# Second cross attention of a two-layer gated block: negated row maxima rounded to bf16 and carried by DMA, copies moved from VectorE to ScalarE, half-transposes and chunks rescheduled, 16 leading matmuls removed

## The reference, cut to what matters

```python
# second cross attention: keys and values from the context, queries from the normalised x
v = values.reshape(N, -1, 16, 16) @ Wv.T
k = keys.reshape(N, 77, 16, 16) @ Wk.T
q = queries.reshape(N, 1024, 16, 16) @ Wq.T
energy = einsum('bqhd,bkhd->bhqk', q, k)
energy = where(mask, energy, -1e20)
attn = softmax(energy / 4, axis=-1)
out = einsum('bhqk,bkhd->bqhd', attn, v).reshape(N, 1024, 256) @ Wo.T + bo
x = x + tanh(g) * out
```

## Time and profile before

| | us |
|---|---|
| median of three runs | 1420.08 |
| lowest and highest | 1419.99, 1422.82 |
| profiled execution, its own time | 1424.06 |
| its span, first to last instruction | 1422.3 |
| TensorE busy, share of the span | 1264.7, 89% |
| VectorE busy | 1044.8, 73% |
| ScalarE busy | 854.3, 60% |
| GpSimd busy | 160.5, 11% |

### The profile page before, as it was taken

One profiled execution on the slowest core, in us unless ns is written; L12 is line 12 of the kernel. 1 busy time (PEld: TensorE's weight loads), 2 busy tenths in 40 slices (PEclk: granted clock), 3 DMA queues, 4 the chain that ended last, 5 costly groups with the idle time before them and its releaser, 6 DMA issues.

```text
span 1422.3 us, 26541 instructions
## 1 busy us (share of the span) xinstructions
PE 1264.7 (89%) x10690; PEld 590.5 (42%) x10690; DVE 1044.8 (73%) x1563; ACT 854.3 (60%) x1432; POOL 160.5 (11%) x139
## 2 busy tenths in 40 slices
PE   4898974899899899948899999999999999999988
PEld 3566662454455755514433233232322333233237
DVE  4897494666664756545699999999999999999802
ACT  2233472666665155511287877887887787887871
POOL 2220021110600223310600000000000000000000
PEclk8977985999999999978799999999999999999999
DMA  5000026444450013340524443323443323443003
GB/s 177 24 1 14 1 29 111 95 85 89 90 90 2 0 67 133 134 94 11 82 50 69 82 79 57 75 54 64 82 81 62 67 56 63 82 81 48 2 1 118
DMA packets 78825, 92.56 MB, mean 65 GB/s; under 512 B 15210, under 2 KB 53356, under 8 KB 78704
## 3 DMA queue, kind: packets, MB, share of 16 engines
q1 hardware_dynamic: 78704, 90.87, 31.6%
HBM read 67.02 MB, written 23.80 MB: 64 GB/s over the span
## 4 chain that ended last, share of the span: by engine, by line
PE 58%; DVE 28%; ACT 7%; issue 4%; DMA 1%; SPq 1%; POOL 1%; DVEq 0%; ACTq 0%; POOLq 0%
DVE sm L1971 18%; PE ps L1460 9%; PE ps L1451 8%; PE ps L1432 6%; PE ps L1351 4%; ACT W L964 3%; PE ps L1216 2%; PE ps L1250 2%; PE ps L1570 2%; PE ps L1167 2%; PE ps L1358 2%; PE ps L1241 2%; PE ps L1299 1%; PE ps L1442 1%; PE ps L1387 1%
## 5 line engine op out<-in xcount | busy, mean ns | idle before, releaser
L1971 DVE TENSOR_REDUCE sm<-ps 128x1 f32<-128x1024 f32 x512 | 599.8, 1218 | 33.1 <-PE ps L1432 29.8
L964 ACT ACTIVATE W<-ps 128x512 f32<-128x512 f32 x1024 | 534.8, 604 | 140.2 <-PE ps L1460 136.3
L1460 PE MATMUL ps<-R 99*32 99x512 bf16 x4096 | 318.5, 383 | 6.2 <-ACT W L964 3.2
L1451 PE MATMUL ps<-W,R 128*32 128x512 f32 x2048 | 266.4, 596 | 0.7 <-ACT W L964 0.7
L1460 PEld LDWEIGHTS ps<-R 99*32 99x32 bf16 x4096 | 86.2, 94 | 225.4 <-ACT W L964 168.5
L882 ACT CAST R<-ps 4x2048 bf16<-4x2048 f32 x32 | 59.5, 1858 | 80.7 <-PE ps L1216 80.7
L1776 DVE TENSOR_REDUCE small<-ps 128x4 f32<-128x308 f32 x128 | 60.9, 477 | 62.6 <-PE ps L1205 62.2
L1432 PE MATMUL ps<-R 50*128 50x512 bf16 x512 | 89.2, 389 | 15.6 <-DVE sm L1971 12.9
L1432 PE MATMUL ps<-KM,R 50*128 50x512 bf16 x512 | 87.2, 384 | 9.6 <-DVE sm L1971 6.6
L1451 PEld LDWEIGHTS ps<-W,R 128*32 128x32 f32 x2048 | 63.2, 111 | 42.5 <-ACT W L964 1.4
L765 POOL COPY R<-R 128x512 f32<-128x512 f32 x16 | 10.3, 644 | 591.7 <-PE ps L1451 591.7
(11 more groups left out here) (258 smaller groups left out, 1587.1 us busy)
## 6 DMA issues: line engine op xcount, KB each, us to landing
R<-x_parts SPq DMA_DIRECT2D x96, 128.0 KB, 4.8
R<-q_parts SPq DMA_DIRECT2D x192, 64.0 KB
R<-q_parts SPq DMA_DIRECT2D x96, 128.0 KB
R<-k_parts SPq DMA_DIRECT2D x96, 128.0 KB
x_parts<-R SPq DMA_DIRECT2D x8, 768.0 KB, 4.1
q_parts<-R SPq DMA_DIRECT2D x24, 256.0 KB, 2.6
k_parts<-R SPq DMA_DIRECT2D x24, 256.0 KB, 2.6
X<-in_x SPq DMA_DIRECT2D x4, 1024.0 KB, 9.8
```

Of the source, the lines that this page charges most:

```text
L964: act.activation(PR[:, s % 2, h, :], third_bank("score", 64 * u + n), ACT.Exp, scale=0.25).then_inc(s_sfree, 1)
L1451: mm = pe.matmul(bank(7)[32 * h:32 * h + 32, :], VST[j][:, k, h, :], PR[:, s % 2, h, :], start=(k == 0), stop=(k == TB - 1))
L1460: mm = pe.matmul(o[32 * c:32 * c + 32, :], KST[j][0:MAX_ROW + 1, h, t:t + 32], QST[j][0:MAX_ROW + 1, h, 512 * (s // 8):512 * (s // 8) + 51 ...
L1971: dve.tensor_reduce(MX[:, half, h, q:q + 1], bank(2 * ((p + 1) % 2), 2), AX, ALU.max).then_inc(s_tfree, 1)
```

## The change

- The negated maxima `Mn` are written as bf16, and `max_transposes1` multiplies them with the bf16 identity in place of the float32 one (four matmuls of 128 columns, as before).
- ScalarE's `max_rows1` copies the 4 x 512 numbers once, to a small double buffer `mrow1`, and then issues four DMAs of 1 KB, each of which brings one head's row to partition 96 of the stack. It waits for its own copy before it issues, and the wait for the stack's readers stands in front of the DMAs. `scores1` waits for the landing of these DMAs (64 on a semaphore of its own) and not for the copy. The stacks have 97 rows in place of 100, and the one-hot rows of `K1s` become one row of ones (one memset in place of four copies on VectorE).
- `copy_out1` moves from VectorE to ScalarE, behind the exponentials and ahead of `max_rows1`.
- On TensorE `max_transposes1(m + 2)` stands ahead of `out_transposes1(m - 2)`.
- The half-transposes of the last eight halves come two steps earlier (steps 0 to 3, 6 to 9, 14 to 17 in place of 0 to 3, 8 to 11, 16 to 19), and three layernorm chunks two steps earlier as well (steps 0, 4, 6, 12, 14 in place of 0, 6, 8, 14, 16).
- The 16 matmuls ahead of the first step are gone.

```diff
-        SR1 = SR + 4
+        SR1 = SR + 1
+        mrow1 = R2f[SR:SR + 4, 5434:5946].bitcast(BF16).rearrange("p (u n) -> p u n", u=2)
-        Mn = small[:, 464:528].rearrange("p (u q j) -> p u q j", u=2, q=8)
+        Mn = small[:, 464:496].bitcast(BF16).rearrange("p (u q j) -> p u q j", u=2, q=8)
+        HALVES = {max(0, 8 * (i // 4) - 2) + i % 4: FIRST + i for i in range(12)}
+        CHUNKS = {0: 3, 4: 4, 6: 5, 12: 6, 14: 7}
...
             def max_rows1(m):
                 act.wait_ge(s_mt, m + 1)
+                if m >= 2:
+                    act.wait_ge(s_mrl[m % 2], 64 * (m // 2))
+                act.copy(mrow1[:, m % 2], bank(2)[SR:SR + 4, :]).then_inc(s_mrc, 1)
                 if m >= 6:
                     act.wait_ge(s_sc, 4 * (m - 5))
-                act.copy(Xs[m // 2 % 3][SR:SR1, :, 512 * (m % 2):512 * (m % 2) + 512],
-                         bank(2)[SR:SR1, :].unsqueeze(1).to_broadcast([4, 4, 512])).then_inc(s_mrc, 1)
+                act.wait_ge(s_mrc, m + 1)
+                for j in range(4):
+                    act.dma_start(Xs[m // 2 % 3][SR:SR1, j, 512 * (m % 2):512 * (m % 2) + 512],
+                                  mrow1[j:j + 1, m % 2]).then_inc(s_mrl[m % 2], 16)
...
+                if m >= 1:
+                    copy_out1(m - 1)
                 if m + 2 < 2 * UNITS:
                     max_rows1(m + 2)
...
-                pe.wait_ge(s_mrc, m + 1)
+                pe.wait_ge(s_mrl[m % 2], 64 * (m // 2 + 1))
...
-            keep_warm(4, 16)
             for m in range(2 * UNITS):
                 scores1(m)
                 if m >= 1:
                     values1(m - 1)
+                if m + 2 < 2 * UNITS:
+                    max_transposes1(m + 2)
                 if m >= 2:
                     out_transposes1(m - 2)
-                if m + 2 < 2 * UNITS:
-                    max_transposes1(m + 2)
...
-            for g in range(4):
-                sel = dve.tensor_copy(K1s[SR:SR1, 4 * g:4 * g + 4, :],
-                                      identB[SR:SR1, SR:SR1].unsqueeze(2).to_broadcast([4, 4, B * KX]))
-            sel.then_inc(s_mk1, 1)
+            dve.memset(K1s[SR:SR1, :, :], 1.0).then_inc(s_mk1, 1)
```

More of the change, by code:

```diff
@@ L247, in build_program @@
         s_mrc = sem("max1_rows")
+        s_mrl = [sem(f"max1_rows_loaded{n}") for n in range(2)]
         s_sc = sem("scores1")
@@ L266, in build_program @@
         FIRST = 4
+        HALVES = {max(0, 8 * (i // 4) - 2) + i % 4: FIRST + i for i in range(12)}
+        CHUNKS = {0: 3, 4: 4, 6: 5, 12: 6, 14: 7}
         def half_in(m):
-            return FIRST + 4 * (m // 8) + m % 8 if m % 8 < 4 and m // 8 + 1 < B else None
+            return HALVES.get(m)
         TURNS1 = []
@@ L879, in max_rows1, with copy_out1 @@
                 act.wait_ge(s_mt, m + 1)
+                if m >= 2:
+                    act.wait_ge(s_mrl[m % 2], 64 * (m // 2))
+                act.copy(mrow1[:, m % 2], bank(2)[SR:SR + 4, :]).then_inc(s_mrc, 1)
                 if m >= 6:
                     act.wait_ge(s_sc, 4 * (m - 5))
-                act.copy(Xs[m // 2 % 3][SR:SR1, :, 512 * (m % 2):512 * (m % 2) + 512],
-                         bank(2)[SR:SR1, :].unsqueeze(1).to_broadcast([4, 4, 512])).then_inc(s_mrc, 1)
+                act.wait_ge(s_mrc, m + 1)
+                for j in range(4):
+                    act.dma_start(Xs[m // 2 % 3][SR:SR1, j, 512 * (m % 2):512 * (m % 2) + 512],
+                                  mrow1[j:j + 1, m % 2]).then_inc(s_mrl[m % 2], 16)
+            def copy_out1(m):
+                act.wait_ge(s_pv, m + 1)
+                if m >= 2:
+                    act.wait_ge(s_ot1, m - 1)
+                act.copy(Oe[:, m % 2], bank(7)).then_inc(s_oc, 1)
             max_rows1(0)
@@ L896, in _ @@
                                    scale=0.25).then_inc(s_e1, 1)
+                if m >= 1:
+                    copy_out1(m - 1)
                 if m + 2 < 2 * UNITS:
                     max_rows1(m + 2)
+            copy_out1(2 * UNITS - 1)
             for c in range(NC):
@@ L1214, in max_transposes1 @@
                 for i in range(4):
-                    mm = pe.matmul(bank(2)[SR:SR1, P * i:P * i + P], Mn[:, m // 2 % 2, 4 * (m % 2) + i, :],
-                                   identF[:, :], start=True, stop=True)
+                    mm = pe.matmul(bank(2)[SR:SR + 4, P * i:P * i + P], Mn[:, m // 2 % 2, 4 * (m % 2) + i, :],
+                                   identB[:, :], start=True, stop=True)
                 mm.then_inc(s_mt, 1)
@@ L1801, in normalise1 @@
                                   rc1.unsqueeze(3).to_broadcast([P, 4, 4, D]), ALU.mult).then_inc(s_on, 1)
[L1803 to L1806, removed]
-                dve.tensor_copy(Oe[:, m % 2], bank(7)).then_inc(s_oc, 1)
             maxima1(0)
@@ L1814, in _ @@
                     maxima1(m + 2, lambda: residue(n, bank_of("half", n)) if n is not None else None)
-                if m >= 1:
-                    copy_out1(m - 1)
-                c = 2 * (m // 8) + {0: 3, 6: 4}.get(m % 8, NC)
-                if c < NC:
-                    ln_chunks(2, [c], lambda c: None)
+                if m in CHUNKS:
+                    ln_chunks(2, [CHUNKS[m]], lambda c: None)
                 if m >= 2:
                     normalise1(m - 2)
-            copy_out1(2 * UNITS - 1)
             normalise1(2 * UNITS - 2)
```

## The result

The changed kernel takes 1483.75 us (median of four runs, 1479.52 to 1485.83) against 1420.03 us for the kernel before on the same chip: a ratio of 1.0443, 95% interval 1.0413 to 1.0473. The prediction of 1405 (1391 to 1433) had the wrong sign; 1483.75 lies 51 us above its range.

A forecast was written before the change was run, and what follows sets the result against it. Bound by TensorE's own sum and, in 12 steps, by when ScalarE comes free. 1424.06 - 21.1 (steps) + 6.5 (landings) - 1.6 (start) + 1.2 (bias adds) = 1409.1, as a median 1405 us, range 1391 to 1433.

The forecast's parts named there:

- The bf16 max-transposes: TensorE's four max-transposes per step: 0.33 us in place of 0.97, 0.64 less; bounds 0.22 and 0.5.
- d: Length of one of ScalarE's four row-DMA issues per step: taken as 0.36 us, bounds 0 and 0.68.
- The two formulas: Step length without a half 3.59 + 4d = 5.03 us, with a half 5.05 + 4d = 6.49; together 21.1 us saved.
- rival (a): ScalarE's queue becomes the bound: at 0.68 an issue, steps cost 0.56 more, about 1437 us; chance 0.17.
- The prediction's own sign: Wrong if exponentials start later than V + 4.5 us, V being the start of a values product; 3.8 was expected.
- The late landings: Row DMAs beside SyncE's stack loads, in 13 steps: slower issues or late landings, 0.5 each, +6.5 us.
- The clock: At the start, step 0 and part of step 1 at 1.2 GHz until about 250: 4.8 us lost, bounds 3 and 11.
- rival (b): The clock stays low: 3.9 us more for each further step at 1.2 GHz, some eight steps give 1436; chance 0.13.
- The start: Without the 16 matmuls, step 0's first product at 241.0, 6.4 us earlier; net -1.6 after the clock loss.
- The bias adds: GpSimd's adds delay VectorE's negation and the clock falls: 8 us carried in place of 6.8, +1.2.
- The rest at nothing: Memset, copy_out1 off VectorE, 97 rows for 100, earlier halves, chunks and part writes: counted as no gain or loss.
- rival (c): Issuing nearly free (at most 0.15 us each): steps fall to 4.92 and about 5.75, 1391 us; chance 0.15.

The follow-up runs named there:

- e1: Changed kernel with the 16 leading matmuls put back: 1479.60 us, 1.0398 of the kernel before.
- e5: Changed kernel without row DMAs; ScalarE copies the maxima under the mask and the mask matmul (100 rows) adds them: 1384.75 us, ratio 0.9759.
- e6: e5 with the 16 leading matmuls put back as well: 1383.55 us, ratio 0.973.
- e8: Kernel before without its 16 leading matmuls, nothing else: 1417.48 us, ratio 0.9983.
- e13: e7 with GpSimd's four bias adds put behind the last negation of the stage: 1402.51 us, ratio 0.987.
- e7: Kernel before with only the negated maxima and max-transposes in bf16: 1432.60 us, ratio 1.0053.
- e10: Changed kernel with the four row DMAs of a step issued by SyncE in place of ScalarE: 1446.20 us, ratio 1.0146.
- e2: Changed kernel with two of the four row DMAs of each step left out: 1449.07 us, ratio 1.017.
- e12: e7 with each of GpSimd's four bias adds cut into eight parts: 1439.94 us, ratio 1.0043.
- e4: Changed kernel with negated maxima and max-transposes back in float32: 1465.34 us, ratio 1.0306.
- e15: e10 with negated maxima and max-transposes in float32: 1427.52 us, ratio 1.0043.
- e17: e7 with the four bf16 max-transposes of a step done four times over: 1424.87 us, ratio 1.0022.
- e16: e7 with the mask matmul over 128 rows in place of 77, the added rows zero: 1407.70 us, ratio 0.9893.
- e18: Changed kernel with the mask matmul over 128 rows in place of 77, the added rows zero: 1454.38 us, ratio 1.0226.
- e14: e6 with GpSimd's four bias adds put behind the last negation of the stage: 1381.55 us, ratio 0.9721.
- e11: e6 with each of GpSimd's four bias adds cut into eight, 32 in all: 1396.71 us, ratio 0.9819.
- e9: Kernel before with four spare 1 KB DMAs issued by ScalarE after each row copy, read by nobody: 1466.43 us, ratio 1.0314.

## Why the prediction was wrong

**The bf16 max-transposes** were sized rightly: 0.39 us in the timeline in place of 1.04, and 0.65 a step in the kernel before against the 0.64 of the sum.

**The issues on ScalarE** are the term that was mis-sized: d is 0.61, not 0.36. The two formulas held: 3.59 + 4d = 6.03 and 5.05 + 4d = 7.49, measured 6.13 and, between ScalarE's row copies, 7.56. (No step with a half ran at 2.4 GHz throughout; from one values product to the next they took 8.3 to 8.7, and more at the start.) What failed was the choice of row: the 0.32 of the earlier trace rows is a single row fetched from DRAM, while one of 1 KB from SBUF to SBUF takes 0.6 on either queue. A nearer row stood in the trace of before, the issues by which SyncE brings rows of 1 KB, four at a time, to a later stage's stacks (L640): 0.56 each, 32 times. The bounds (0 to 0.68) held it. At 2.4 GHz this is, as an estimate from these steps, 18 x 0.39 + 12 x 0.38 = 11.6 us slower than before in place of 21.1 faster, a turn of 33 us. It is rival (a), to which I gave 0.17, and whose 1437 still lies 47 us under the result. The prediction's own sign for it came: the first exponential starts 4.9 us after V, beyond the 4.5 that it named as wrong.

**The late landings** cost 5.7 us of waits, against 6.5 in the sum, but not where the sum had them: 3.8 are at the start, and the three waits in later steps come to 1.9. That the totals are close is luck. Their consequence for the clock was not in the sum. The rule cited in the prediction (the Trainium skill, "DMA: Bandwidth & Descriptors", Issuing engines are not separate DMA queues) agrees with the trace: the first rows took up to 7.2 us and landed only as the last of the stack loads issued ahead of them did, and the longest landing is 7.1 from SyncE. That section calls the sequencer's time "usually small relative to the DMA itself"; here it is 0.61 of a median 2.2, four times a step, and it is the sequencer that bounds the step.

**The clock** is the rest. 48 us were lost in the stage; 11.6 are the issues, and the other 36 are steps at 1.2 GHz and waits. The price of such a step was right: 8.82 against 8.9. Wrong was what I let it hang on. I tied the half clock to the start and the missing 16 matmuls, and counted one to three such steps. Three pairs with and without those matmuls (the changed kernel and e1, e5 and e6, before and e8) differ by about 4 us or less. Two other things decide. First, idle gaps of 0.5 to 2.6 us (3.8 at the start) came back in most steps that were not at half clock anyway, since ScalarE was late in them; that a gap can start the half clock is shown by e13 against e7 for the one behind the negation, 26 to 30 us, and is carried over to these. Second, the change took away part of the work that lifts the clock again. With bf16 max-transposes and a mask matmul of 77 rows the clock stayed at half for seven steps at the end of the changed kernel, seven in e10, six in e2 and in e7, eight in e12; in e7 and e1 it came back in the end without a change in the work. With float32 transposes (e4, e15), with bf16 ones repeated (e17), or with the mask matmul of 100 or 128 rows (e5, e16, e18) it was back within about two. e16 and e18 change nothing but rows of zeros, and give 25 and 29 us. Of the 36 us in the stage e18 gives back 20 (its row copies run from 235.5 to 467.4), and 5 more behind the stage. The other 16 are the gaps and the shorter stretches at 1.2 GHz behind them, which no run divides further.

The prediction had the piece in hand: in rival (b), "the transposes at the end of a step are what preceded the rise there" stood as an argument against, and it wasn't seen that the change shrinks those very transposes from 1.87 us at half clock to 0.59.

The Trainium skill ("TensorE: Matmul & The Clock Gate", Part 1) has activity release the throttle. These runs narrow that: a fully busy TensorE didn't release it over 63 us (428 to 491 in the changed kernel), and with rows of zeros added (e18) the longest stretch at half from 250 on was 7 us.

**The start**: the first product at 245.19 in place of 241.0, since the rows landed 3.77 us after TensorE was ready, and the clock back near 273 in place of 250. By the first values product the changed kernel is 1.2 us behind (258.40 against 257.23), by the third 6.1 (277.00 against 270.90); the sum had it 1.6 ahead. Of the late start the row DMAs are the cause, not the missing matmuls: with these back (e1) the first steps are 3.79, 10.91, 9.48 and 10.3 against 3.78, 11.12, 9.48 and 10.23, and without the DMAs (e5) they are 3.79, 7.16, 6.36 and 5.3. The clock alone does not make these steps: in e1 it was up from 244 to 254, in e18 from 247.5 to 254, and it fell again behind the next wait of 2.2.

**The bias adds**: I expected 8 us for 6.8. The changed kernel hardly waits there (0.8), because its longer steps leave cover. The mechanism was right, however, and mattered most where steps are short: 8.41 us of stall in e5's profiled execution, and 26 to 30 us in e7 against e13.

**The rest at nothing** held in the changed kernel: without row DMAs (e5) the remaining change, with the mask matmul of 100 rows, gives some 35 us, more than the 21.1 of my steps, as ScalarE's copy is 0.58 in place of 1.86 and steps fall to 4.68 and 5.74, close to rival (c)'s 4.92 and 5.75. One reason given for it fails once steps are that short: the stack of unit 4 is late then (e5, e13, e14), and costs some 7 us in e5.

## To carry to other kernels

A DMA issue is an instruction on its engine's path: count issues times their measured length for that kind of transfer, and ask whether they can start beside the work in front of them or must wait for it. Where TensorE is the bound, an idle gap costs itself and may cost the steps at 1.2 GHz behind it: remove the stalls first, and before making its work smaller look at which work stood before each rise of the granted clock; zeros in the unused rows of a matmul may give it back. Data that a matmul can add on the way (rows under a mask) need not travel. After each step that is made shorter, ask which load was in time only because the step was long.

## What the runs showed of the hardware that was not expected

- An issue of a 1 KB transfer within SBUF takes 0.61 us on ScalarE and 0.59 on SyncE (median of 128), beside 0.32 for one row of 1 KB from DRAM early in the kernel before, 0.56 for four such rows in its later stage (L640) and 0.43 for one of 128 KB in this stage.
- An issue that waits for nothing runs beside the engine's own instruction: 2.43 us of issues beside a cast of 1.86 (e9).
- TensorE can be fully busy at a granted clock of 0.50 for 63 us, and with the mask matmuls over 128 rows in place of 77, 380 ns either way, the clock is back within about two steps: 25 us in e16, 29 in e18.
- A tiny negation on VectorE (128 x 16) can be held up by GpSimd's SBUF operations: it took 3.83 us in the kernel before, 9.16 in e5, and 13.09 when the adds were cut into 32. The Trainium skill ("SBUF — State Buffer", SBUF: two separate sides) has the engine that starts first hold the shared pair of ports "for the whole instruction". The negation of 3.83 agrees: it ends at 383.87, where one add follows another (383.84). The rule alone does not give the longer two: in e5 the negation waited through two adds and in e11 through some nineteen short ones, while another negation in e11 passed between two of them in 0.49.
